# Sixteen-head attention in periods of two heads: scores from stacked halves with copied operands, new orders on every engine, and GpSimd splitting the pair's products

## The reference

```
q = einsum('qdh,bcd->bhcq', Q, x) * sq        # 16 heads of width 64
k = einsum('qdh,bcd->bhcq', K, x) * sq
v = einsum('vdh,bcd->bhcv', V, x) * sv
att = where(causal, einsum('bhcq,bhCq->bhcC', q, k) / d_query, -inf)
p = softmax(att)
y = einsum('bhcC,bhCv->bhcv', p, v)
z = einsum('dvh,bhcv->bcd', W, y) * (sqrt(d_embed / d_value) / num_heads)
```

## Time and profile before

| | |
|---|---|
| median of 3 runs | 1520.9 us (1517.05 to 1522.49) |
| profiled execution | 1514.62 us, span 1512.6 us |
| busy, share of the span | TensorE 86%, VectorE 73%, ScalarE 62%, GpSimd 50% |
| mean granted TensorE clock | 0.921 |
| DMA traffic | 64.47 MB, mean 43 GB/s |

### The profile page before, as it was taken

How to read it: one execution, slowest core, us unless ns; L and a number is a source line. 1 busy time by engine, 2 the same in 40 slices (tenths; PEclk the granted TensorE clock), 3 DMA queues, 4 the chain that set the end, 5 groups by cost and what they waited for, 6 DMA issues and landing times. The chain is left out here.

```text
span 1512.6 us, 28432 instructions
## 1 busy us (share of the span) xinstructions
PE 1302.4 (86%) x8377; PEld 1111.3 (73%) x8377; DVE 1100.1 (73%) x2826; ACT 941.5 (62%) x2522; POOL 760.4 (50%) x950
## 2 busy tenths in 40 slices
PE   1587635999669999999999999999999998299992
PEld 1476534999648888888888888888888886199991
DVE  5666544777548888888887887888888887277773
ACT  1554422444348878888788888888787886054440
POOL 3005563444325555576575675665765665434443
PEclk9986657999869999999999999999999999599996
DMA  9391011222100000000000000000000000022215
GB/s 181 125 375 36 29 39 50 61 59 62 29 30 11 2 15 1 1 26 5 3 24 5 4 26 1 22 8 1 8 8 1 12 5 4 29 61 62 60 52 172
DMA packets 91936, 64.47 MB, mean 43 GB/s; under 512 B 34020, under 2 KB 77935, under 8 KB 91792
## 3 DMA queue, kind: packets, MB, share of 16 engines
q1 hardware_dynamic: 78928, 43.65, 10.8%
q0 software_dynamic: 8640, 16.93, 3.5%
q10 hardware_dynamic: 4224, 2.10, 0.5%
HBM read 26.59 MB, written 36.96 MB: 42 GB/s over the span
## 5 line engine op out<-in xcount | busy, mean ns | idle before, releaser
L1366 POOL TENSOR_TENSOR b_probs<-b_probs,b_recip 128x128 f32<-128x128 f32 (+3 forms) x512 | 352.7, 719 | 307.2 <-DVE b_recip L1599 307.2
L420 DVE TENSOR_TENSOR b_pt_lo<-b_ring,b_pt_hi 128x512 fp32r<-128x512 f32 (+1 forms) x384 | 219.1, 598 | 93.1 <-ACT b_pt_hi L414 87.8
L545 ACT ACTIVATE b_probs<-b_s_bank,b_neg_max 128x256 f32<-128x256 f32 (+3 forms) x512 | 267.9, 533 | 27.7 <-DVE b_neg_max L537 26.3
L537 DVE TENSOR_REDUCE b_neg_max<-b_s_bank 128x1 f32<-128x256 f32 (+3 forms) x512 | 219.7, 479 | 47.8 <-PE b_s_bank L529 46.8
L1227 POOL DMA_INDIRECT y_rows<-f_y_sb,f_dest x142 | 139.1, 979 | 192.7 <-DVE f_y_sb L1200 185.0
L414 ACT ACTIVATE b_pt_hi<-b_ring 128x512 fp32r<-128x512 f32 (+1 forms) x384 | 192.2, 547 | 9.5 <-PE b_ring L485 8.6
L485 PE MATMUL b_ring<-ident,b_probs 128*128 128x128 f32 x1280 | 179.3, 278 | 4.8 <-DVE b_q_lo L420 4.8
L81 PE MATMUL b_s_bank<-b_k_hi,b_q_hi 64*128 64x256 f32 (+3 forms) x512 | 180.6, 353 | 2.9 <-ACT b_probs L545 1.4
L1170 ACT ACTIVATE f_hid_hi<-f_hid_bank 128x384 fp32r<-128x384 f32 x142 | 69.9, 492 | 160.1 <-PE f_hid_bank L1123 142.1
L82 PE MATMUL b_s_bank<-b_k_lo,b_q_hi 64*128 64x256 f32 (+3 forms) x512 | 164.4, 321 | 0.0
L83 PE MATMUL b_s_bank<-b_k_hi,b_q_lo 64*128 64x256 f32 (+3 forms) x512 | 163.8, 320 | 0.0
(11 more groups left out here) (304 smaller groups left out, 3345.2 us busy)
## 6 DMA issues: line engine op xcount, KB each, us to landing
x_sorted<-a_blank SPq DMA_DIRECT2D x64, 260.0 KB, 3.9
f_xs<-x_sorted SPq DMA_DIRECT2D x142, 65.0 KB
b_yc<-y_rows SPq DMA_DIRECT2D x16, 256.0 KB, 3.2
f_yc<-y_rows SPq DMA_DIRECT2D x16, 256.0 KB, 5.1
y_rows<-f_y_sb,f_dest POOLq DMA_INDIRECT x142
x_tok<-in_L_attn_a_x_dram SPq DMA_DIRECT2D x8, 256.0 KB, 4.6
out_dram<-x_tok ACTq DMA_DIRECT2D x8, 256.0 KB, 5.3
f_raw<-in_L_ffn_W_dram SPq DMA_DIRECT2D x1, 1408.0 KB, 6.7
```

The source lines that it names most:

```text
L420: nc.vector.tensor_tensor(dst, src(rg.of(key)), hi.bitcast(F32), ALU.subtract).then_inc(rg.lo_done, 1)
L537: nc.vector.tensor_reduce(sc.neg_max[:, i:i + 1], s_tile(sc, i), AX.X, ALU.max, negate=True).then_inc(sc.max_done, 1)
L545: nc.scalar.activation(probs[:, P_AT[i]:P_AT[i] + (i + 1) * P], s_tile(sc, i), ACT.Exp, bias=sc.neg_max[:, i:i + 1], accum_out=sums[:, i:i ...
L1366: nc.gpsimd.tensor_tensor(part, part, recip[:, i:i + 1].to_broadcast([P, (i + 1) * P]), ALU.mult).then_inc(probs_done, 1)
```

## The change

1. **Stacked scores.** A new tile per half of a pair, `stack[0]` for even heads and `stack[1]` for odd ones, holds three slots of 512 columns on 128 partitions: slot 0 is q high over q low, slot 1 is k high twice, slot 2 is k low twice. A head's scores are two passes over 128 rows, slot 0 by slot 1 and slot 0 by slot 2, in place of three over 64 rows; low by low is added. The stacks are filled by SyncE with three copies a head, from the tile `qk` that now holds q and k.
2. **Periods.** Every engine's loop goes over pairs ("periods") and has a new order in which the even and the odd head differ; the scores of a head are spread over the period. Steps of the sequences that come and leave move to new places, several of them now in one piece, and the scatters come as three, three and two in one period.
3. **Tile order.** `S_GROUPS` becomes `((3,), (2,), (1, 0))`, in both attentions.
4. **GpSimd** makes the high part of y as well as the low part.
5. **Memory.** `xn` shares the second buffer of the experts' rows, `xn_t` of the routing shares `z`, and `over` shares `apart`.

The core of the diff:

```diff
-S_GROUPS = ((1, 0), (2,), (3,))
-S_AT = {1: (0, 0), 0: (0, 2 * P), 2: (1, 0), 3: (2, 0)}
-S_READ = (2, 3, 4)
+S_GROUPS = ((3,), (2,), (1, 0))
+S_AT = {3: (0, 0), 2: (1, 0), 1: (2, 0), 0: (2, 2 * P)}
+S_READ = (1, 2, 4)
...
-        q = (sb("q_hi", [P, T], F32R), sb("q_lo", [P, T], F32R))
-        k = (sb("k_hi", [P, T], F32R), sb("k_lo", [P, T], F32R))
+        qk = sb("qk", [P, 4, T], F32R)
+        q, k = (qk[:, 0, :], qk[:, 3, :]), (qk[:, 1, :], qk[:, 2, :])
+        stack = [sb(f"stack{i}", [P, 3, T], F32R) for i in range(2)]
+        stack_in = [sem(f"stack_in{i}") for i in range(2)]
...
         @block.sync
+            def rows_of(b):
                 wait(sp, yc_added, b)
+                if b:
+                    ring_filled(sp, rg, ("xn", b - 1))
...
+            def stacked(u):
+                pair, half = divmod(u, 2)
+                rows = qk[half * KD:half * KD + KD].bitcast(F32)
+                to = stack[half][:].bitcast(F32)
+                sp.wait_ge(rg.lo_done, rg.lo["k", pair])
+                wait(sp, sc.s_full, (u - 1) * len(S_GROUPS))
+                sp.dma_start(to[0:KD, :, :], rows[:, 0:3, :]).then_inc(stack_in[half], 16)
+                sp.dma_start(to[KD:P, 0, :], rows[:, 3, :]).then_inc(stack_in[half], 16)
+                sp.dma_start(to[KD:P, 1:3, :], rows[:, 1:3, :]).then_inc(stack_in[half], 16)
+            rows_of(0)
+            for u in range(NU):
+                stacked(u)
+                if u == 0:
+                    rows_of(1)
+                b, h = divmod(u, NH)
+                if h == 2 * TURNED + 2 and b + 2 < NB:
+                    rows_of(b + 2)
...
         @block.gpsimd
+            def y_high(pair):
+                pool.wait_ge(y_done, 2 * pair + 2)
+                wait(pool, z_full, pair)
+                nc.gpsimd.tensor_copy(y_parts[0][:], y[:]).then_inc(y_hi_done, 1)
...
+            def sent(p):
+                b, i = p // PERIODS - 2, p % PERIODS
+                if 0 <= b < NB - 1 and i < SENT:
+                    for j in range(SENT * i, min(NK * QT, SENT * i + SENT)):
+                        route_scatter(nc, pool, g, rt, b, j)
+            for p in periods:
+                if paired(p - 2):
+                    y_high(p - 2)
+                    y_low(p - 2)
...
+                if paired(p):
+                    divide(2 * p)
+                    divide(2 * p + 1)
+                sent(p)
...
         @block.tensor
             def scores(u, group):
-                rows = slice(u % 2 * KD, u % 2 * KD + KD)
+                if group == 0:
+                    pe.wait_ge(stack_in[u % 2], (u // 2 + 1) * 3 * 16)
                 s_free(pe, sc, u, group)
                 for i in S_GROUPS[group]:
-                    st = [part[rows, i * P:i * P + P] for part in q]
-                    mv = [part[rows, 0:(i + 1) * P] for part in k]
-                    three_passes(nc, s_tile(sc, i), st, mv, i == S_GROUPS[group][0], False)
+                    for part in (1, 2):
+                        nc.tensor.matmul(s_tile(sc, i), stack[u % 2][:, 0, i * P:i * P + P],
+                                         stack[u % 2][:, part, 0:(i + 1) * P],
+                                         start=(i == S_GROUPS[group][0] and part == 1), stop=False)
...
+            for p in periods:
+                even, odd = 2 * p, 2 * p + 1
+                scores(even, 0)
+                masks((even - 1, 2), (even, 0))
+                if paired(p):
+                    values(p)
+                products(even - 3)
+                transposes(even - 2)
+                scores(even, 1)
+                scores(even, 2)
+                masks((even, 1), (even, 2))
+                if paired(p + 1):
+                    project("q", g.b_q, p + 1)
+                scores(odd, 0)
+                if paired(p + 1):
+                    project("k", g.b_k, p + 1)
...
+                products(even - 2)
+                scores(odd, 1)
+                masks((odd, 0), (odd, 1))
+                transposes(odd - 2)
+                if paired(p - 2):
+                    output(p - 2)
+                scores(odd, 2)
...
         @block.scalar
+            for p in range(NU // 2 + PERIODS):
+                even, odd = 2 * p, 2 * p + 1
+                transposed(even - 2, 0)
+                transposed(even - 2, 1)
+                exponentials(even, 0)
+                transposed(even - 2, 2)
+                exponentials(even, 1)
+                if paired(p + 1):
+                    for copied in stack_in:
+                        act.wait_ge(copied, (p + 1) * 3 * 16)
+                    split_hi(nc, act, rg, ("q", p + 1), q[0])
+                    split_hi(nc, act, rg, ("k", p + 1), k[0])
...
+                exponentials(even, 2)
+                y_half(even - 2)
+                transposed(odd - 2, 0)
+                exponentials(odd, 0)
+                transposed(odd - 2, 1)
+                transposed(odd - 2, 2)
+                exponentials(odd, 1)
+                if paired(p + 1):
+                    values_hi(p + 1)
+                exponentials(odd, 2)
+                y_half(odd - 2)
...
         @block.vector
+            for p in periods:
+                even, odd = 2 * p, 2 * p + 1
+                maxima(odd - 2, 2)
+                maxima(even, 0)
+                if paired(p):
+                    hi, lo, bank = v_parts(p)
+                    split_lo(nc, dve, rg, ("v", p), lo, hi, bank)
+                inverse(odd - 2)
+                y_sum(odd - 4)
+                transposed(even - 2, 0)
+                transposed(even - 2, 1)
+                maxima(even, 1)
+                transposed(even - 2, 2)
+                maxima(even, 2)
+                if paired(p + 1):
+                    for copied in stack_in:
+                        wait(dve, copied, (p + 1) * 3 * 16)
+                    split_lo(nc, dve, rg, ("q", p + 1), q[1], q[0])
+                    split_lo(nc, dve, rg, ("k", p + 1), k[1], k[0])
...
+                maxima(odd, 0)
+                inverse(even)
+                maxima(odd, 1)
+                transposed(odd - 2, 0)
+                y_sum(even - 2)
+                transposed(odd - 2, 1)
+                transposed(odd - 2, 2)
```

More of the change, by code:

```diff
@@ L1336, in _ @@
         def _(sp):
-            for b in range(NB):
+            def rows_of(b):
                 wait(sp, yc_added, b)
+                if b:
+                    ring_filled(sp, rg, ("xn", b - 1))
                 for i in range(NK):
@@ L1377, in _ @@
+            for j in range(NK * QT):
                 route_scatter(nc, pool, g, rt, NB - 1, j)
@@ L1408, in scores, with transposes @@
+            def transposes(u):
+                if alive(u):
+                    pe.wait_ge(probs_done, u * QT + QT)
+                    for i in range(len(PT_BANKS)):
+                        head_transpose(nc, pe, rg, turns(u), probs[u % 2], i, g.ident)
             def scores(u, group):
-                if u % 2 == 0 and group == 0:
-                    pe.wait_ge(rg.lo_done, rg.lo["k", u // 2])
-                rows = slice(u % 2 * KD, u % 2 * KD + KD)
+                if not alive(u):
+                    return
+                if group == 0:
+                    pe.wait_ge(stack_in[u % 2], (u // 2 + 1) * 3 * 16)
```

330 lines of the change are left out of this document (143 added, 187 removed).

## The result

The changed kernel takes 1731.9 us (median of 4 runs, 1728.3 to 1732.5), the kernel before 1519.5 beside it: ratio 1.139, 95% interval 1.136 to 1.142. The forecast was 1572 us, the range 1485 to 1660: slower, as forecast, but four times as much, 212 us in place of 51, and outside the range. The profiled execution has a span of 1730.5 us.

The account below looks back on a forecast made before the run. TensorE was taken as the bound; with copies, the even-head loop of 8.99 + 4.9 us makes a 13.89 us period, 0.73 more. 63 periods give 46 us, the start 5: 1520.9 + 51 = 1572 us, range 1485 to 1660.

Parts of the forecast that it names:

- Matmuls taken away: TensorE's scores: the third pass goes, 1.28 us a period, at most 82 us gained.
- Copies added, and where they stand: Loop from even head's score through k and copies to the next even head's score: 8.99 us plus D a period.
- D: Time of a head's three copies on SyncE's queue: taken as 4.9 us, bounds 3.6 and 6.2.
- signs named: Profile after: 13.9 us period, even-head wait about 1.9 us, none at odd head, TensorE busy time down about 80 us.
- the sum's loop at full clock: TensorE's even-head loop: 8.99 us beside the copies, 13.89 us a period with them, 46 us more over 63 periods.
- third rival: TensorE's clock falls after waits; two microseconds at 1.2 GHz add 126 us, 1700 us; shares 30% with half-width copies.
- The first rival: Half-width copies share ports: D up to 6.2, period 16.2 us, 1718 us; 30% together with a fallen clock.
- The rest of the change: Other engines' moved work, tile order, GpSimd's high part, masks and shared buffers: nothing in the sum.
- VectorE's pieces: VectorE's normalisation and routing chains in one piece, up to 2.6 us: hidden at 13.9 us, up to 20 us at 11.9.
- the fast case: D under 3.0, TensorE the bound again: period 11.9 us, 1441 to 1466 us with VectorE's pieces and GpSimd's scatters.
- second rival: Copies are short and the change is faster: 1489 us at D = 3.6, down to 1441 under 3.0; 26%.
- Sum: Whole kernel: 46 us for the periods plus 5 at the start on a median of 1520.9, giving 1572 us.

Follow-up runs that it names:

- g1_three_early: Changed kernel with three score passes over 64 rows, no stacks or copies, and VectorE's two once-per-sequence blocks earlier in its period: 1568.6 us, ratio 1.033.
- f2_nc_early: Changed kernel with only the first two heads' stacks filled, no later copies, and VectorE's two once-per-sequence blocks moved to mid-period: 1496.5 us, ratio 0.992.
- e5_warm: Changed kernel with 20 small matmuls on TensorE ahead of the even head's wait for its copies: 1714.6 us, ratio 1.137.
- e1_full_width: Changed kernel with each head's three copies made 256 KB over all 128 partitions, same total bytes: 1622.4 us, ratio 1.067.
- e2_other_half: Changed kernel with the second and third copy of a head reading the other half of the partitions: 1736.8 us, ratio 1.142.
- e4_no_copies: Changed kernel with only the first two heads' stacks filled and reused by all later heads, no copies in the loop: 1580.0 us, ratio 1.039.
- h2_cover_early: Changed kernel with TensorE's v, product and transposes ahead of the even head's first scores, and VectorE's two once-per-sequence blocks earlier: 1547.5 us, ratio 1.022.
- i1_drain: Changed kernel with four copies a head, TensorE work ahead of scores, blocks earlier, and a transposed tile's low part ahead of two VectorE maxima: 1542.8 us, ratio 1.016.
- three-pass kernel: Changed kernel with stacks undone, three score passes over 64 rows from two buffers of q and k, no copies: 1726.5 us, ratio 1.144.

## Why the prediction was wrong

**Matmuls taken away: right.** At most 82 us were put on the third pass; 63 were measured between g1_three_early and f2_nc_early.

**Copies added, and where they stand: right as a mechanism.** The forecast loop was 8.99 us + D, at full clock. With the clock up e5_warm shows 9.28. Of the signs named, the wait at the even head is there (2.6 us in the mean of 59, against 1.9), and next to none at the odd head; the third copy lands at 4.3 us, against 4. The copies before the first score cost 6 us, against 5. Two signs came out otherwise: the granted clock of the stage is 0.89, which was named as a sign of being wrong, and TensorE's busy time fell by 16 us (1302.4 to 1286.5) and not by 80, since much of its work ran at half clock.

**First failed step, the sum's loop at full clock: the largest part of the miss.** The forecast had no fall of the clock in its sum, only in the third rival. From an even head's score to the next pair's first copy 10.48 us pass in the mean of 56 periods, and not 8.99. About 0.98 us of the difference are the clock (10.26 against 9.28 in the medians, e5_warm); waits of TensorE for a bank of the ring, 30.5 us in all or 0.48 a period, come to about the rest. The prediction argued that 13 of 14 us would stay busy, and did not ask what the wait of 1.9 us that it forecast would do each time. Its third rival named the mechanism, with two microseconds of work a period at 1.2 GHz; that is about what the 4 us stretch holds, but only half of it lengthens the loop. Removing the fall by itself gave back little, as e5_warm shows.

**Second, the size of D: mis-sized.** Taken 4.9, measured 5.63 in the mean. I chose the row of the tail's loads as the nearest. It shared queue and bytes with the copies, but not the width, and e1_full_width shows that the width decides; the upper bound, half of the best rate on the page over one half of the partitions, gave 6.2, about as far off on the other side. If 2 us are taken off for issue and landing (a 32 KB copy took 2.1), 768 KB (786 thousand bytes) in 3.63 us are an estimated 217 GB/s. The Trainium skill, "SBUF — State Buffer", on the DMA port swizzle, gives some 196 to 218 GB/s for 64 partitions, and this case agrees; by its figure the prediction had D at 5.5. That copies from two halves don't add, which e2_other_half shows for three copies on SyncE's queue, was also read from it, from its section on two DMAs to the two halves.

**The first rival's number, partly luck.** Half-width copies were priced at a period of 16.2 us and 1718 us, close to 16.41 and 1732; I gave this 30% together with the clock. Half width is right, but the 16.2 held 6.2 for D and 1.0 for an odd head that comes late. D is 5.63, the odd head is hardly ever late, and the clock, which that sum left out, fills the place of both. The range ended at 1660, below this rival's own 1718.

**The rest of the change: the third failed step.** "VectorE's pieces" were put at nothing in a period of 13.9 us and at up to 20 us in the fast case. I compared their length with VectorE's idle time, and not the place of their last instruction with whoever waits for it: the z bank's first writer on TensorE, and the rstd on GpSimd, behind which the divides stand. f2_nc_early against e4_no_copies: 71 us. (Tile order and GpSimd's high part, 616 ns in the mean of 61, were put at nothing too, rightly as far as the kernel before shows; the masks were not tested by themselves.) The second rival, too, fell by this: had the copies cost nothing at all, the kernel would still be 3.9% slower, and not at 1441 to 1489 us.

**Sum.** The period is 2.52 us above the forecast (16.41 against 13.89). The loop gives 1.49 of it (10.48 less 8.99), D 0.73 (5.63 less 4.9), and the longer once-per-sequence periods the 0.30 that are left: 94, 46 and 19 us over 63 periods, and with the 1 us more at the start the whole 160 us by which 1572 missed. Taken out one at a time from the changed kernel, the copies give 152 us back and the blocks 12; taken out together, (1.139 - 0.992) x 1519 = 223. Part of each lies in the other's shadow.

**What is left open:** the 33 us of h2_cover_early over the kernel before. The trace has them in waits of about 1 us between TensorE, VectorE and ScalarE in each period, and i1_drain shows that a change of place only moves them. Whether a longer ring or more score banks would take them was not tried, nor were the scatters in threes or the other moved steps of the sequences undone by themselves.

## What to carry to other kernels

A row of a copy is near only if its width in partitions is the same; the same bytes over half the partitions landed in 3.8 us where the full width took 2.4. When a wait is forecast for an engine whose clock can fall, put the fall into the sum, and not into a rival. When work is gathered into a block, ask for each engine that waits for its last instruction what else is queued behind that wait; the block's length against the idle time says nothing on this. Where TensorE is full, a wait costs more than its own length, since the clock falls behind it (52 us of waits less gave 169 us in the three-pass kernel). And of two costs on one loop, the smaller one shows only when the larger is gone, so take both out before naming what the change can bring.

## What the hardware showed

- Copies within the chip's buffers, three per head on SyncE's queue, 768 KB: landing 3.8 us in the median over 64 partitions, 2.4 over 128; by size over 64 partitions, 3.6 for 384 KB, 3.7 for the 128 KB behind it, 4.3 for the 256 KB behind both.
- A wait of 1.17 us was followed by a stretch of some 7 us at the 1.2 GHz level (records of 512 columns of 0.79 us from 1024.27 on, three-pass run), one of 4.37 us by more than 16 us of it, although TensorE was busy 16.00 of 16.00 us; in the changed kernel, waits of 3 us are followed by some 4 us. These few cases do not show what sets how long the clock stays down.
- An issue by SyncE of a 256 KB copy at line 1352 takes 467 to 1838 ns, median 1217; the one of 384 KB at line 1350, first in its turn, 461 to 607.
